# Graph attention: row groups of four, two, one and one blocks in place of four, three and one, with single-unit transfers for the last two groups

## The reference

```python
h = maximum(layernorm(x), 0)                 # x: 4096 x 128 float32
H = h @ W + b                                # W: 128 x 128
s_src = H @ w_att[:128]; s_dst = H @ w_att[128:]
scores = s_src[:, None] + s_dst[None, :] + b_att
scores = where(A > 0, scores, -1e9)          # A: 4096 x 4096 int32, zeros and ones
out = x + softmax(scores, axis=1) @ H
```

## Time and profile before

| what | value |
|---|---|
| time, median of 3 runs | 186.21 us (185.15 to 186.57) |
| profiled execution, its own time | 186.24 us |
| its span | 184.3 us |
| busy: PE, PEld, DVE, ACT, POOL | 160.3, 115.3, 124.9, 79.6, 10.7 us |
| mean granted TensorE clock | 0.97 |
| DMA moved | 71.63 MB, mean 389 GB/s |

### The profile page before, as it was taken

The page is one execution under the profiler, slowest core; times in us unless marked ns, Lnnn a source line. Parts: engine busy times, 40 slices in busy tenths (PEclk is TensorE's granted clock), DMA queues, the critical chain, the costliest instruction groups (busy, mean ns, idle before and its releaser), DMA issues.

```text
span 184.3 us, 2691 instructions
## 1 busy us (share of the span) xinstructions
PE 160.3 (87%) x866; PEld 115.3 (63%) x866; DVE 124.9 (68%) x360; ACT 79.6 (43%) x232; POOL 10.7 (6%) x33
## 2 busy tenths in 40 slices
PE   0639859989499999989899999999999998999970
PEld 0326638666386867656668667686786775887750
DVE  0995696947999556788865569496594624459931
ACT  2567894999395052222251422442224424021020
POOL 2103601000130020000000000000000000000000
PEclk9999987999969999999999999999999999999995
DMA  5999999999999999999999999999999999998212
GB/s 144 410 439 432 412 443 420 434 420 430 427 430 432 412 441 411 441 420 428 420 422 424 427 427 424 422 427 423 425 424 427 437 431 427 411 398 329 76 60 59
DMA packets 8369, 71.63 MB, mean 389 GB/s; under 512 B 929, under 2 KB 1698, under 8 KB 3490
## 3 DMA queue, kind: packets, MB, share of 16 engines
q1 hardware_dynamic: 7776, 71.18, 92.3%
q10 hardware_dynamic: 578, 0.26, 0.5%
HBM read 69.34 MB, written 2.10 MB: 388 GB/s over the span
## 4 chain that ended last, share of the span: by engine, by line
DMA 59%; PE 23%; DVE 10%; issue 2%; ACT 2%; SPq 1%; DVEq 0%
DMA ring<-adj 59%; PE bank L844 9%; PE bank L850 8%; DVE mask L514 5%; PE bank L868 3%; PE bank L892 2%; PE bank L882 1%; DVE low L537 1%; ACT mask L456 1%; DVE mask L523 1%; ACT weighted L363 1%; SPq L271 1%; DVE x_sb L639 1%; DVE x_sb L646 1%; SPq L277 0%
## 5 line engine op out<-in xcount | busy, mean ns | idle before, releaser
L514 DVE TENSOR_SCALAR mask<-ring 128x1024 fp32r<-128x1024 int32 (+2 forms) x69 | 63.1, 934 | 41.6 <-DMA ring<-adj 37.1
L844 PE MATMUL bank<-mask,high 128*128 128x512 f32 x256 | 80.7, 418 | 11.0 <-DVE mask L514 6.3
L850 PE MATMUL bank<-mask,low 128*128 128x512 f32 x256 | 76.3, 401 | 0.0
L844 PEld LDWEIGHTS bank<-mask,high 128*128 128x128 f32 x256 | 47.8, 196 | 31.1 <-DVE mask L514 12.9
L850 PEld LDWEIGHTS bank<-mask,low 128*128 128x128 f32 x256 | 49.8, 194 | 11.1
L456 ACT ACTIVATE mask<-ring,half_steep 128x512 fp32r<-128x512 int32 x43 | 28.9, 718 | 62.1 <-DMA ring<-adj 60.6
L868 PE MATMUL bank<-mask,w_cols 128*32 128x512 bf16 x256 | 19.7, 392 | 2.3 <-ACT lines L422 2.3
L868 PEld LDWEIGHTS bank<-mask,w_cols 128*32 128x32 bf16 x256 | 5.9, 94 | 13.1 <-issue 8.7
L363 ACT ACTIVATE weighted<-relu,w_over_std 128x128 f32<-128x128 f32 x32 | 10.1, 391 | 4.7 <-DVE w_over_std L608 4.5
L374 ACT ACTIVATE relu<-x_sb,neg_mean 128x128 f32<-128x128 f32 x32 | 9.8, 388 | 3.2 <-DVE neg_mean L546 3.2
L389 ACT ACTIVATE high<-x_sb,neg_mean 128x128 fp32r<-128x128 f32 x24 | 9.3, 387 | 0.0
(11 more groups left out here) (85 smaller groups left out, 67.7 us busy)
## 6 DMA issues: line engine op xcount, KB each, us to landing
ring<-adj SPq DMA_DIRECT2D x18, 2048.0 KB, 17.1
ring<-adj SPq DMA_DIRECT2D x16, 1536.0 KB, 12.9
ring<-adj SPq DMA_DIRECT2D x3, 1024.0 KB, 9.3
out<-x_sb SPq DMA_DIRECT2D x7, 256.0 KB, 13.8
x_sb<-x SPq DMA_DIRECT2D x1, 1024.0 KB, 20.7
ring<-adj SPq DMA_DIRECT2D x4, 256.0 KB, 16.2
x_sb<-x SPq DMA_DIRECT2D x2, 256.0 KB, 3.8
x_sb<-x SPq DMA_DIRECT2D x1, 512.0 KB, 10.1
```

Of the source, the lines that this page charges most:

```text
L514: nc.vector.tensor_scalar(mask[:, n % MASKS, 0:cols], ring[:, n // 2 % RING, begin:begin + cols], 0.0, None, ALU.is_gt).then_inc(masks_rea ...
L844: nc.tensor.matmul(bank[:, b, :], high[:, t, :], mask[:, n % MASKS, cols], start=(t == 0), stop=False)
L850: last = nc.tensor.matmul(bank[:, b, :], low[:, t, :], mask[:, n % MASKS, cols], start=False, stop=(t == T - 1))
```

## The change

The groups become `[(0, 4), (4, 2), (6, 1), (7, 1)]`. A unit of width 2 takes two tiles, so every unit is 4 pieces and there are 64 units: 0 to 31 group 0, 32 to 47 group 1, 48 to 55 group 2, 56 to 63 group 3. The sums stand in banks 0 to 3, then 0 and 1, then 2, then 3. Pairs 24 to 30 (units 48 to 61, groups 2 and 3 without the last pair) are loaded as two transfers of one unit each, with a semaphore for each half. The steps between the masks and the sums are placed anew, and the bias is added at units 32 to 35 (a chunk each), 45 and 49 (two chunks each), with a semaphore on which `result_of` waits.

```diff
-GROUPS = [(0, 4), (4, 3), (7, 1)]
+GROUPS = [(0, 4), (4, 2), (6, 1), (7, 1)]
+SUM_BANKS = [[0, 1, 2, 3], [0, 1], [2], [3]]
+HALVED = range(24, 31)
...
-        step = 4 if width == 1 else 1
+        step = 4 // width
...
-    SHARED = [n for n, u in enumerate(UNITS) if 20 <= n < LAST and n - FIRST[u[0]] >= 4]
+    SHARED = [n for n, u in enumerate(UNITS) if 20 <= n < LAST and n - FIRST[u[0]] >= (4 if u[0] < 2 else 2)]
+    def bank_free(g, b):
+        for before in range(g - 1, -1, -1):
+            if SUM_BANKS[g][b] in SUM_BANKS[before]:
+                return banks_before(before) + SUM_BANKS[before].index(SUM_BANKS[g][b]) + 1
+        return 0
...
+                if pair in HALVED:
+                    for i in range(2):
+                        half = slice(i * cols // 2, (i + 1) * cols // 2)
+                        sp.dma_start(ring[:, pair % RING, half], adj_g[g][t0 // (2 * step)][:, half]).then_inc(half_landed[pair % RING][i], 16)
...
+            nc.gpsimd.memset(pick_two[:], 0.0).then_inc(cleared, 1)
...
+                nc.gpsimd.memset(pick_two[rows, q % 2:q % 2 + 1], 1.0).then_inc(pick_set, 1)
...
             def result_of(g, b, done):
+                dve.wait_ge(bias_added, k + 1 if k < PER else 5 if k < 6 else 6)
...
-                if n in range(36, 36 + CHUNKS):
+                chunks = {32: [0], 33: [1], 34: [2], 35: [3], 45: [4, 5], 49: [6, 7]}.get(n, [])
...
# VectorE, group 1: mean_wide, mean_H with inverse_of(0), results of group 0, path
-                    if local == 4:
+                    if local == 2:
...
-                    if local == 8:
+                    if local == 4:
...
-                    if local in (14, 17, 20, 23):
-                        result_of(0, (local - 14) // 3, results_ready)
-                    if local == 26:
+                    if local in (6, 8, 10, 12):
+                        result_of(0, (local - 6) // 2, results_ready)
+                    if local == 14:
...
                 if g == 2:
+                    if local == 2:
+                        inverse_of(1)
+                    if local in (3, 5):
+                        result_of(1, (local - 3) // 2, results_ready)
+                if g == 3:
+                    if local == 2:
+                        inverse_of(2)
                     if local == 3:
-                        inverse_of(1)
-                    if local in (4, 5):
-                        result_of(1, local - 4, results_ready)
+                        result_of(2, 0, results_ready)
...
-            result_of(1, 2, results_ready)
...
# TensorE, group 1: the mean (L914) at local 0, mean_H (L917) at local 2
-                    if local in (10, 12, 16, 18):
-                        products(0, {10: 0, 12: 1, 16: 2, 18: 3}[local])
+                    if local in (4, 6, 8, 10):
+                        products(0, (local - 4) // 2)
                 if g == 2:
                     if local == 0:
                         den_columns(1)
                         products(1, 0)
-                        products(1, 1)
-                    if local == 4:
-                        products(1, 2)
+                    if local == 2:
+                        products(1, 1)
+                if g == 3:
+                    if local == 0:
+                        den_columns(2)
+                        products(2, 0)
```

More of the change, by code:

```diff
@@ L42, in units_of, with gnn_kernel @@
     for g, (_, width) in enumerate(GROUPS):
-        step = 4 if width == 1 else 1
+        step = 4 // width
         out += [(g, t, step) for t in range(0, tiles, step)]
     return out
-def gnn_kernel(nc, x, adj_0, adj_1, adj_2, adj, w_fc, w_fc_t_and_a, b_a_b_att, out):
+def gnn_kernel(nc, x, adj_0, adj_1, adj_2, adj_3, adj, w_fc, w_fc_t_and_a, b_a_b_att, out):
     N, D = x.shape
@@ L103, in gnn_kernel @@
         pick = sb("pick", [P, 4], F32)
+        pick_two = sb("pick_two", [P, 2], F32)
         half_steep = sb("half_steep", [P, 1], F32)
@@ L179, in gnn_kernel @@
         pair_landed = [sem(f"pair_landed{c}") for c in range(RING)]
+        half_landed = [[sem(f"half_landed{c}_{i}") for i in range(2)] for c in range(RING)]
         next_to_last_landed = sem("next_to_last_landed")
@@ L215, in gnn_kernel @@
         products_done = sem("products_done")
+        bias_added = sem("bias_added")
         results_ready = sem("results_ready")
@@ L253, in unit_landed @@
                 engine.wait_ge(first_landed[n], 16)
+            elif pair in HALVED:
+                engine.wait_ge(half_landed[pair % RING][n % 2], 16 * ((pair - HALVED.start) // RING + 1))
             elif n == LAST - 1:
@@ L256, in unit_landed @@
             else:
-                engine.wait_ge(pair_landed[pair % RING], 16 * (pair // RING + (pair % RING > 0)))
+                whole = [p for p in range(1, pair + 1) if p % RING == pair % RING and p not in HALVED]
+                engine.wait_ge(pair_landed[pair % RING], 16 * len(whole))
         block = ctx.enter_context(nc.Block())
@@ L283, in _ @@
                     slot_free(pair)
-                sp.dma_start(ring[:, pair % RING, 0:cols], adj_g[g][t0 // (2 * step)]).then_inc(pair_landed[pair % RING], 16)
+                if pair in HALVED:
+                    for i in range(2):
+                        half = slice(i * cols // 2, (i + 1) * cols // 2)
+                        sp.dma_start(ring[:, pair % RING, half], adj_g[g][t0 // (2 * step)][:, half]).then_inc(half_landed[pair % RING][i], 16)
+                else:
+                    sp.dma_start(ring[:, pair % RING, 0:cols], adj_g[g][t0 // (2 * step)]).then_inc(pair_landed[pair % RING], 16)
                 if pair == 2:
@@ L329, in _ @@
             pool.wait_ge(a_wide_ready, 1)
-            pool.wait_ge(cleared, 4)
+            pool.wait_ge(cleared, 5)
             for q in range(4):
-                nc.gpsimd.memset(pick[32 * q:32 * q + 32, q:q + 1], 1.0).then_inc(pick_set, 1)
-            pool.wait_ge(pick_set, 4)
+                rows = slice(32 * q, 32 * q + 32)
+                nc.gpsimd.memset(pick[rows, q:q + 1], 1.0).then_inc(pick_set, 1)
+                nc.gpsimd.memset(pick_two[rows, q % 2:q % 2 + 1], 1.0).then_inc(pick_set, 1)
+            pool.wait_ge(pick_set, 8)
             nc.gpsimd.affine_select(out=ident[:], in_=ident[:], compare_op=ALU.not_equal, fill=1.0, base=0,
@@ L635, in result_of @@
                 k = b0 + b
+                dve.wait_ge(bias_added, k + 1 if k < PER else 5 if k < 6 else 6)
                 for m in range(PER):
                     row = x_sb[:, k * PER + m, :]
-                    at = m * width + b
-                    last = nc.vector.scalar_tensor_tensor(out=row, in0=mean_H[:], scalar=is_empty[:, g, at:at + 1], in1=row,
+                    at = b0 * PER + m * width + b
+                    last = nc.vector.scalar_tensor_tensor(out=row, in0=mean_H[:], scalar=is_empty[:, at:at + 1], in1=row,
                                                           op0=ALU.mult, op1=ALU.add)
@@ L719, in _ @@
                     link(nc.vector.tensor_reduce(v_square[:], product[:], AX_X, ALU.add))
-                if n in range(36, 36 + CHUNKS):
-                    rows = x_sb[:, (n - 36) * PER:(n - 35) * PER, :]
-                    nc.vector.tensor_tensor(rows, rows, b_row.unsqueeze(1).to_broadcast([P, PER, D]), ALU.add)
+                chunks = {32: [0], 33: [1], 34: [2], 35: [3], 45: [4, 5], 49: [6, 7]}.get(n, [])
+                for c in chunks:
+                    rows = x_sb[:, c * PER:(c + 1) * PER, :]
+                    last = nc.vector.tensor_tensor(rows, rows, b_row.unsqueeze(1).to_broadcast([P, PER, D]), ALU.add)
+                if chunks:
+                    last.then_inc(bias_added, 1)
                 if n in range(23, 23 + CHUNKS):
@@ L840, in sums @@
                     for b in range(width):
-                        if g > 0 and t == 0:
-                            pe.wait_ge(sums_copied, banks_before(g - 1) + b + 1)
+                        if t == 0 and bank_free(g, b) > 0:
+                            pe.wait_ge(sums_copied, bank_free(g, b))
                         cols = slice((i * width + b) * BLOCK, (i * width + b + 1) * BLOCK)
-                        nc.tensor.matmul(bank[:, b, :], high[:, t, :], mask[:, n % MASKS, cols],
+                        nc.tensor.matmul(bank[:, SUM_BANKS[g][b], :], high[:, t, :], mask[:, n % MASKS, cols],
                                          start=(t == 0), stop=False)
@@ L849, in sums @@
                         cols = slice((i * width + b) * BLOCK, (i * width + b + 1) * BLOCK)
-                        last = nc.tensor.matmul(bank[:, b, :], low[:, t, :], mask[:, n % MASKS, cols],
+                        last = nc.tensor.matmul(bank[:, SUM_BANKS[g][b], :], low[:, t, :], mask[:, n % MASKS, cols],
                                                 start=False, stop=(t == T - 1))
@@ L875, in den_columns @@
                 width = GROUPS[g][1]
-                rows = 32 * width if width > 1 else P
```

(7 more changed lines are left out.)

14 lines of the change are left out of this document (6 added, 8 removed).

## The result

| | before | changed |
|---|---|---|
| time, median | 186.01 us (185.15 to 186.57, 8 runs) | 187.41 us (186.95 to 187.87, 8 runs) |
| ratio to before | | 1.0079 (1.0058 to 1.0099) |
| profiled execution, its span | 186.24, 184.3 us | 187.67, 185.5 us |
| last sums end | 176.70 | 177.69 |
| tail behind them | 7.6 | 7.8 |

The forecast was 185.5 us, 0.4% faster; it is 0.8% slower, and outside the range (183.5 to 187.0).

What follows compares the result with a forecast made beforehand. TensorE, with a backlog of 5 us behind the loads, was taken to bound the end; 2.9 us gained less 2.2 us of stalls gave -0.7, from 186.24 to 185.5 us, range 183.5 to 187.0.

Steps and rivals of the forecast that it cites:

- rival B: End of the kernel: the loads, not TensorE, set the end, giving 180.9 us; chance 0.05.
- The pieces: TensorE's work summed from parts, two matmuls (0.456 us) a piece: group 1 39.4, group 2 19.7, group 3 18.8 us.
- The idling at unit 64: Start of old group 2: TensorE's 0.79 us wait for a landing, with a 0.27 slow matmul behind it, would go.
- D: Loads of groups 2 and 3: transfers by halves cost rate; about 188.5 us if it matters; chance 0.02.
- C, the handshake of the mean: Start of group 1: TensorE waits for VectorE's copies of mean and mean_H, up to +3.6 us, 189.1; chance 0.12.
- The new waits: Group 1: VectorE waits for products before masking the odd unit, so TensorE stalls, 2.0 us plus 0.2 slow start.
- The first round: Unit 39 in group 1: set by the landing of pair 19, ready at 113.4, wanted at 112.7, 0.7 us late.
- The other three: The three later rounds in group 1, up to unit 45: some 0.2 us each, 0.6 together.
- Units 46 and 47 with the slow start: End of group 1: bias chunks and path chain delay the masks, 0.7 us; slow matmuls behind stalls, 0.2.
- The bound for the slow start behind a stall: Group 1: a matmul behind idling is slow by 0.27 us; six stalls give 0 to 1.6, 0.2 taken.

Runs made afterwards that it cites:

- the run without stalls: Changed kernel with group 0's results, mean_H, inverse_of(0) and path chain one unit later, bias chunks 4 and 5 at unit 47: 183.86 us, ratio 0.9900.

## Why the prediction failed

**What held.** TensorE bounds the end, not the loads (rival B fell: a TensorE freed of 3.4 us of stalls ended its sums earlier by as much, 174.30 against 177.69). The pieces held: 39.4 for group 1 in the run without stalls, 19.75 and 19.0 for groups 2 and 3 against 19.7 and 18.8. No unit waits at the start of group 3. The idling at unit 64 was worth 0.9 to 1.0 us, and halves show no gain behind a backlog of TensorE. The regrouping itself is a gain of about 1 us, where its pieces gave 1.5 (two passes less, one `den_columns` more): 183.86 against 185.10, both with halves and both without the new stalls, is 1.2, and by the ratios to the kernel before (0.9900 and 0.9946) it is 0.9. D fell with the whole pairs: seven transfers fewer left the time as it was (187.26 against 187.41), so no price of a single transfer shows where they are queued. C, the handshake of the mean, turned out small: unit 37 starts 2.20 behind unit 36, 0.4 late.

**The step that failed** is in "The new waits": "1.13 + 0.96 - 1.83 = 0.26 a round, some 0.2 with the overlap of neighbours". The mechanism and its place were right; the term was mis-sized by a factor of three. A round costs 0.62 us by the comparison with the results one unit later. Term by term, with the restart of 0.06 that is paid anyway, it is 0.68: 0.35 that products need, once TensorE has started its next matmul, until VectorE can start on them; 1.04 and 0.96 for the L672 and the mask; some 0.05 back to TensorE; less 1.83; and 0.11 because TensorE runs slowly for its first matmuls behind a wait. I had let VectorE start at the moment at which TensorE went on, and in these rows it starts 0.35 us later. All stalls of group 1 were put at 2.0 + 0.2; they are 42.8 - 39.4 = 3.4. The first round was put at 0.7 and is about 0.6. The other three were put at 0.6 together and are 1.9. Units 46 and 47 with the slow start were put at 0.9, and they and unit 37, at which no stall was counted, take the other 0.9. By the medians, the results' share is 2.8 (187.41 to 184.61), that of the other three steps 1.1 (187.41 to 186.35) and both together 3.55. The lengths of group 1 in the traces (42.8, 40.6 and 39.4) give the results 2.2 of the 3.4. The medians were taken at different times, with the kernel before at 185.84 to 186.12, so the shares hold to some tenths only.

**The rest of the miss.** The last sums came at 177.69 and not 176.0: 1.2 of it is the stalls, 0.25 the pieces of groups 2 and 3, and 0.26 a later entry into group 1 (96.1 against 95.86). That last part isn't explained. The masks that begin when pair 15 has landed, 89.60 before and 89.87 changed, began between 89.47 and 89.95 in six of the profiles, so it may be no more than the spread of single executions; it wasn't tried. The profiled execution, 187.67, is 2.2 above the forecast: 1.7 in the last sums, 0.2 in the tail and 0.2 outside the span. Its median lies 0.26 below it.

**What the forecast said of its own weak point** was right: it hung on 2.2 us of stalls against 2.9 gained. The bound for the slow start behind a stall reached 1.6 us, and 0.2 was taken without a row that spoke for it. The 0.27 a stall behind that bound was misread: the matmul of the earlier trace rows was slow because it follows a pass of denominators, as the kernel before with halves shows. The latency too could have been read off the kernel before. Its timeline of TensorE has the matmuls that follow the mean and mean_H:

```profile
103.72 0.94 PE L844 MATMUL bank<-mask,high 128*128 128x512 f32 x3
...
110.60 0.94 PE L844 MATMUL bank<-mask,high 128*128 128x512 f32 x3
```

VectorE's copies of the two, for which it was waiting, begin at 104.00 and 110.88, 0.28 us behind. With that in three rounds (+0.8) and 0.11 behind each of six stalls (+0.5) the forecast would have been 186.8: slower, the right way, and still 0.9 short of the profiled execution.

## What to carry to other kernels

When a step of an in-order engine waits for another engine's result, write down the loop from start to start, with the latency between the producer's going on and the consumer's start as a term of its own, and compare it with the work that the producer has in hand meanwhile. Put such a step behind everything that the other engine will need next: here, moving the results, the mean and the path chain by one unit and two bias chunks by two turned 0.8% slower into 1.0% faster, with the same instructions. And ask of finer transfers whether the reader is waiting at all: halves were worth 1.0 us in one kernel and nothing that shows in the other.

## What the runs showed of the hardware

Here a wait of TensorE costs more than its length. The first group of matmuls behind one took 0.56 us up to the next where 0.46 is usual, although the granted clock was 1.00. It isn't the wait alone that does it: behind `products`, with no wait, the same group takes 0.54 (117.51 to 118.05). From the start of the matmul behind `products` VectorE started on their result 0.35 us later (117.51 to 117.86). The idle time in a row of the profile understates such a wait (0.33 for 0.57), since modelled ends overlap the next start.

In the run with the results one unit earlier TensorE was busy 7.06 of 11 and 4.83 of 7 us with the clock at 1.00; then the granted clock fell to a mean of 0.57 for four us, just while TensorE was fully busy again. So in that run the waits of 2.4 us each were followed by 1.6 us more that no wait shows. That they are its cause is not shown: no run changes the waits alone around that stretch, though no other profile here shows such a fall in group 1.
